# Writing a kernel's fp16 matmuls as quadruples of 32 stationary columns: a two-layer transformer on one core

## What is computed

```
attention 1: q = x Mq, k = x Mk (8 heads of 64), v = x Mv (8 heads of 32)
             out = softmax(q k^T / 8) v
ffn 1:       y = silu(fq(x) wg^T) * (fq(x) wu^T);  out = fq(y) wd^T
             fq rounds blocks of 16 numbers to a 4-bit float with a scale of their own; 704 hidden columns
attention 2: qkv = x W + b, 16 heads of 16; q and k are normalised per head;
             out = softmax(q k^T / 4) v, projected by w_proj, plus a bias
ffn 2:       x W^T + b, plus a mixture of 8 experts of rank 16 of which each row takes two
```

## Time and profile before

| | |
|---|---|
| median of 3 runs | 3107.68 us (3097.03 to 3111.84) |
| the profiled execution | 3096.75 us, of which the span of its instructions 3095.0 us |
| mean granted TensorE clock | 0.965 of full speed |
| PE busy | 2695.8 us (87%), 23,854 matmuls and as many weight loads |
| VectorE, ScalarE, GpSimd busy | 69%, 63%, 42% |

### The profile page before, as it was taken

How to read it: one execution, slowest core, us unless ns; L and a number is a source line. 1 busy time by engine, 2 the same in 40 slices (tenths; PEclk the granted TensorE clock), 3 DMA queues, 4 the chain that set the end, 5 groups by cost and what they waited for, 6 DMA issues and landing times.

```text
span 3095.0 us, 62688 instructions
## 1 busy us (share of the span) xinstructions
PE 2695.8 (87%) x23854; PEld 1235.7 (40%) x23854; DVE 2138.9 (69%) x4363; ACT 1961.1 (63%) x3701; POOL 1297.9 (42%) x1645
## 2 busy tenths in 40 slices
PE   4875787999899988999889988999889998899796
PEld 2433443335433444334433354334443444333232
DVE  6878766847787577866678487875778666775533
ACT  3541355885577755876568755776558765687683
POOL 4752375216632366224652166323662156511211
PEclk9987998999999999999999999999999999999898
DMA  4212241414223232224324242233322342222311
GB/s 125 61 20 53 50 102 38 81 38 109 50 58 71 59 92 59 69 46 81 88 58 81 44 104 49 66 62 66 92 62 62 43 88 68 61 64 42 86 28 28
DMA packets 474718, 201.33 MB, mean 65 GB/s; under 512 B 287753, under 2 KB 464401, under 8 KB 474393
## 3 DMA queue, kind: packets, MB, share of 16 engines
q1 hardware_dynamic: 472120, 195.12, 29.2%
q10 hardware_dynamic: 2272, 1.85, 0.2%
HBM read 46.61 MB, written 32.51 MB: 26 GB/s over the span
## 4 chain that ended last, share of the span: by engine, by line
PE 50%; DVE 24%; ACT 7%; issue 7%; POOL 4%; DMA 4%; SPq 4%; DVEq 0%; ACTq 0%; POOLq 0%
PE pV L649 10%; PE pR L433 8%; DVE nmaxa L1130 7%; PE pS L497 7%; PE pR L434 6%; PE pR L435 6%; PE pS L620 6%; ACT ub L874 5%; PE pV L530 4%; PE pR L439 2%; SPq L1797 2%; DMA xT<-xhb 1%; POOL ua L1590 1%; DVE ua L1042 1%; ACT ua L835 1%
## 5 line engine op out<-in xcount | busy, mean ns | idle before, releaser
L874 ACT ACTIVATE ub<-pS 128x512 f32<-128x512 f32 x2048 | 1047.7, 612 | 240.2 <-PE pS L620 237.2
L1130 DVE TENSOR_REDUCE nmaxa<-pS 128x1 f32<-128x1024 f32 x512 | 620.9, 1213 | 338.4 <-PE pS L497 337.6
L835 ACT ACTIVATE ua<-pS,nmaxa 128x1024 f32<-128x1024 f32 x384 | 427.6, 1113 | 515.1 <-DVE nmaxa L1130 507.4
L1590 POOL TENSOR_SCALAR ua<-ua,rz 128x256 f32<-128x256 f32 x512 | 493.3, 964 | 497.2 <-DVE rz L1147 458.9
L497 PE MATMUL pS<-ua 128*128 128x512 f16 x2048 | 543.6, 390 | 92.2 <-ACT ua L835 76.4
L649 PE MATMUL pV<-ub,vaug 128*17 128x512 f32 x4096 | 541.0, 599 | 8.8 <-DVE ub L1281 8.8
L620 PE MATMUL pS<-ub 50*128 50x512 f16 x1920 | 350.6, 385 | 26.6 <-DMA ub<-scr 11.5
L530 PE MATMUL pV<-ua 128*32 128x128 f32 x6144 | 255.8, 287 | 53.6 <-DVE oTa L1141 33.4
L497 PEld LDWEIGHTS pS<-ua 128*128 128x128 f16 x2048 | 165.0, 99 | 337.2 <-ACT ua L835 109.9
L835 ACT ACTIVATE EA<-pS,nmaxa 128x1024 f32<-128x1024 f32 x128 | 142.6, 1114 | 169.4 <-DVE nmaxa L1130 169.4
L620 PEld LDWEIGHTS pS<-ub 50*128 50x128 f16 x1920 | 86.6, 94 | 393.5 <-ACT ub L874 324.4
(11 more groups left out here) (289 smaller groups left out, 5157.3 us busy)
## 6 DMA issues: line engine op xcount, KB each, us to landing
ua<-ua SPq DMA_DIRECT2D x384, 128.0 KB, 2.6
ub<-scr SPq DMA_DIRECT2D x264, 64.0 KB, 2.6
scr<-ub SPq DMA_DIRECT2D x30, 512.0 KB, 3.2
x<-in_L_attn_x SPq DMA_DIRECT2D x8, 1024.0 KB, 5.4
between<-x SPq DMA_DIRECT2D x7, 1024.0 KB, 5.2
ub<-between SPq DMA_DIRECT2D x7, 1024.0 KB, 5.9
out<-ub SPq DMA_DIRECT2D x7, 1024.0 KB, 5.2
ub<-scr SPq DMA_DIRECT2D x192, 32.0 KB, 1.9
```

The lines of the kernel that those rows point to most:

```text
L835: e.activation(EA[n % 4], pS[:, 1024 * (n % 2):1024 * (n % 2) + 1024], ACT.Exp, bias=nmaxa[:, n % 32:n % 32 + 1], accum_out=zz[:, n % 8:n ...
L874: e.activation(EB[(4 * n + hl) % 8], pS[:, 512 * hl:512 * hl + 512], ACT.Exp).then_inc(e1_in, 1)
L1130: e.tensor_reduce(nmaxa[:, n % 32:n % 32 + 1], pS[:, 1024 * (n % 2):1024 * (n % 2) + 1024], AXX, ALU.max, negate=True).then_inc(max0_in, 1)
L1590: e.tensor_scalar(vs[m % 4], vv[:, :, 32 * c:32 * c + 32], rz[:, c:c + 1], None, ALU.mult).then_inc(vs_in, 1)
```

## The change

`mm3` and the scores of the first attention call a new helper, which writes each matmul as four: the stationary operand's 128 columns in four slices of 32, each with the whole moving operand, each into the 32 partitions of the result that belong to its slice. The semaphore is raised by the fourth. What is computed stays the same. The scores of the second attention (line 620), the values (lines 530 and 649, which have this form already) and the fp32 transposes (line 439) are not touched. Nor are waits, buffers, the other engines or the order of the lanes.

```diff
+            def by_columns(dst, w, m, start, stop):
+
+                for j in range(0, 128, 32):
+                    i = e.matmul(dst[j:j + 32], w[:, j:j + 32], m, start=start, stop=stop)
+                return i
+
             def mm3(dst, w, m, start=True, stop=True):
-                e.matmul(dst, w[0], m[0], start=start, stop=False)
-                e.matmul(dst, w[0], m[1], start=False, stop=False)
-                return e.matmul(dst, w[1], m[0], start=False, stop=stop)
+                by_columns(dst, w[0], m[0], start, False)
+                by_columns(dst, w[0], m[1], False, False)
+                return by_columns(dst, w[1], m[0], False, stop)
...
-                                i = e.matmul(pS[:, at:at + 512], ka[:, c, o:o + 128],
-                                             qq[:, 4 * jh:4 * jh + 4, o:o + 128], start=(w_ == 0), stop=(w_ == 1))
+                                i = by_columns(pS[:, at:at + 512], ka[:, c, o:o + 128],
+                                               qq[:, 4 * jh:4 * jh + 4, o:o + 128], w_ == 0, w_ == 1)
```

## The result

The changed kernel takes 3078.17 us (median of 7 runs, 3070.78 to 3087.28), beside 3108.35 us for the kernel before (7 runs, 3097.03 to 3114.80): 30 us less, a ratio of 0.9908 with a 95% interval of 0.9887 to 0.9928. The forecast was 3050. The direction is right and the value lies in the range, but only half of the 58 us came. The profiled execution took 3082.79 us with a mean granted clock of 0.959 of full speed (before: 3096.75 us at 0.965).

What follows compares the result with a forecast made beforehand. PE was taken to lead, busy for 87% of the span, but not alone. 3096.75 - 58 = 3039 us for an execution like the profiled one; the median stands 11 us above, so 3050, range 3002 to 3100.

Steps and rivals of the forecast that it cites:

- Removed: changes of form: Between PE's matmuls of different form: net 1090 changes vanish, net 916 of them unhidden, 0.105 us each, 96 us.
- The rival that the changes stay: PE's form hangs on more than the 32 columns, so changes cost as now: 3108; 0.14 together with another engine taking over.
- Added: matmuls, issue, weight loads: On PE: 26,304 more matmuls and as many weight loads; four go at the pace of one, cost taken as nothing.
- The rival of the sequencer: Issue paces PE's products above 27 ns a pair: 3386 at 51 ns; 0.12 together with fetch or strips not overlapping.
- What of it is on the path: Net 551 of the vanished changes lie where the chain runs from PE piece to PE piece: 58 us gained.
- if PE's idle time grows by what the gaps lost: Sign on PE's timeline that would show the prediction wrong: the time the gaps give up returns as idle time.
- The case that another engine takes over: PE arrives earlier and waits for maxima, exponentials or transfers: 0 to 15 us gained; 0.14 together with the changes staying.
- Clock: "taken as unchanged": PE's clock, 1.00 and 0.97 in the stretches read, was taken to stay as it was, at no cost.
- Instruction fetch: "hidden by fetching ahead": Instruction packets grow from 3.39 MB to some 7 MB, with the fetch hidden and costing nothing.
- the bound of 200: If instruction fetch is not hidden, some 200 more packets cost up to 0.96 us each, about 200 us.

Runs made afterwards that it cites:

- 64 columns: Changed kernel with pairs of 64 stationary columns instead of quadruples of 32: 3114.06 us, ratio 1.0042 to the kernel before.
- 50 rows: Changed kernel with the second attention's 50-row scores written as four matmuls too: 3080.29 us, ratio 0.9931 to the kernel before.
- lean kernels: Kernel before without the middle of three matmuls in some products: 3075.04 us (second halves' projections and qkv), 3086.58 us (first halves' gate and up).
- filler: Changed kernel with four more value matmuls in each step of the first attention, into pV columns nobody reads: 3114.91 us, ratio 1.0031 to the kernel before.
- The scores alone: Kernel before with only the first attention's scores written as four matmuls, mm3 left whole: 3110.50 us, ratio 1.0027.
- short maxima: First attention's maxima taken over 512 of the 1024 columns: 2970.89 us in the kernel before, 2969.59 us in the changed kernel.

## Why the prediction was half right

**Removed: changes of form.** Right. 1090 net changes vanished, as counted; they took 106 us of PE's time by starts, about 0.1 us each. The forecast's 96 us were for those that no wait hides; like with like, 931 fewer of these (forecast 916) and 96 us. The experiments with 64 columns and with 50 rows show that it is the form, in rows and in columns, and not the split; 17 and 32 columns, fp16 and fp32, share one. The rival that the changes stay is out. The Trainium skill says as much without a size: its page TensorEngine Tiling (Array Packing), Tiling Modes, has switching modes drain the array; the trace agrees, with 0.09 to 0.10 us from the last column to the next start.

**Added: matmuls, issue, weight loads.** Right: sets at 0.108, 0.15 and 0.215 us. The rival of the sequencer is out. The 62 ns for a matmul that the Trainium skill gives for decoding by microcode (TensorE: Matmul & The Clock Gate, Part 2) are not what this trace shows: a set of four at 256 columns, with its four weight loads, is over in 108 ns.

**What of it is on the path.** This is the step that failed: "Net 551 x 0.105 = 58 us", the share of 0.6 of the chain. The chain names one holder for each moment; it does not tell how close the next one is. The share meant that 0.6 of each microsecond that PE saves (58 of 96) leaves the run; measured, it was 30 of 96, 0.31. The lean kernels measured the exchange with no new form in play: 0.5 in first halves, 0.37 outside of them, and the filler 0.30. Of the 106 us, 29 lie in the first halves (by starts, 120.6 to 91.4 over seven of them) and 77 elsewhere: 0.5 x 29 + 0.37 x 77 = 43 us, by the intervals of the two shares 34 to 52; if only the 96 unhidden ones count, some 39. The prediction did name what would be late next, and said it would be wrong "if PE's idle time grows by what the gaps lost"; that is what happened, 89 us of 106 (17 of the 89 by name only). The case that another engine takes over was thus the nearer description, with more left than its 0 to 15 us.

**Clock: "taken as unchanged".** It failed in size. The mean over the runs went from 0.963 to 0.961 (0.960 when run again), some 4 to 7 us by the slope of 1.9 us per 0.001, and in one of the stretches shown the clock fell from 0.99 to 0.96 and the stretch got longer.

**Instruction fetch: "hidden by fetching ahead".** Mostly. It is 412 packets as forecast (6.75 MB). One stop of 0.5 us before became 8 stops of 4.8 us in all, far from the bound of 200, and not the nothing that was taken.

**The opening**, which the prediction did not treat by itself, lost 7 us up to the second attention in the profiled execution. The kernel before with leaner first halves lost 5.5 there with its opening unchanged up to 229.7 us, so this is only in part the form's, if at all. Against the 30 us measured (22 to 35 by the interval) the exchange gives 34 to 52, and less 4 us of fetch stops 30 to 48: the two meet at the lower end. The clock can't be taken off once more, since the lean kernels' shares hold their own loss of clock (0.9605 in the first halves' kernel). And the shares rest on kernels that left out other time than the change's gaps, so this is a rough agreement in size, not a proof.

**Open.** The scores alone cost 7 us while they free 36 us of PE. With short maxima the change is worth about nothing though PE holds 54% of the chain; the starts show where it is lost (opening and joints), for one pair of executions. That PE's freed time turns into waits is seen, what decides how much of it does was not isolated. Nor was the clock followed moment by moment: that it falls when PE is relieved rests on the means of the kernels and on the filler, and one lean kernel does not show it.

## What to carry to other kernels

Count where neighbouring matmuls differ in rows or columns of the array, and if PE has no wait there, give them one form: each change is worth 0.1 us of PE here, and four strips of 32 columns keep the pace of one matmul. Before putting a price on PE's time, leave some matmuls out of the kernel and measure: here 0.37 to 0.5 us came back for each (and 0.30 was lost for each that was added), though PE was busy for 87% and held half of the chain. Where PE waits anyway the new form has nothing to give and still adds instructions to fetch; keeping the old one in the opening was, by the medians, worth 10 us here, likely but not certain.

## What the runs showed of the hardware

- A fetch of instructions can stop PE inside a step, away from any wait; in the changed kernel, too, after ten of sixteen values (timeline of PE, then the queue that fetches instructions in 1241 to 1243 us):

```profile
1242.43 0.60 PE L536 MATMUL pV<-ua 128*32 128x128 f32 x10
1244.27 0.42 PE L536 MATMUL pV<-ua 128*32 128x128 f32 x6 [1.23 <-issue]
```

```profile
q8 instruction: 1, 0.02, 2.9%
```

  The distance of 2.2 to 2.7 us was what the stops were looked for by (8 in this kernel with 412 packets). It is borne out by the stops that name no wait and left PE idle for over 0.3 us: all three in this kernel and all eight in the one with short maxima began again 2.2 to 2.7 us after the start of such a packet, though the packets came only every 7.5 us.
- The mean granted clock differed from kernel to kernel: 0.9586 (scores only), 0.9605 (matmuls left out, first halves), 0.961 (the change), 0.9627 (matmuls left out, second halves), 0.963 (before; also the changed kernel with short maxima), 0.964 (filler), 0.965 (64 columns), 0.973 (before, with short maxima). It does not simply follow PE's work: the kernel with 83 us less of it stands beside the kernel before. With executions of one kernel 1.9 to 2.5 us went with each 0.001.
- Runs of 64-column pairs start slower than others: 0.173 us for the first step of 352 columns, beside 0.160 for a whole matmul.
